# Three rounded products and centred weights in the expert up-projection of an RWKV and mixture-of-experts block

## What is computed

```python
# block 1: RWKV attention, per batch
key, value, rec = x mixed with x shifted by one token, three mixes
k, v = key @ Wk, value @ Wv
r = sigmoid(rec @ Wr)
rwkv = wkv(time_decay, time_first, k, v)      # a scan over the 512 tokens
x1 = layernorm(x + (r * rwkv) @ Wo)
# block 2: 8 experts of 16 hidden units, the best 2 of them per token
gate = softmax(x1 @ router_w.T) * top2_mask
a = silu(x1 @ down_w.T)                       # 128 hidden units per token
out = layernorm(x1 + (a * gate) @ up_w)       # up_w as a 128 x 512 matrix
```

## Time and profile before

| | |
|---|---|
| time, median of 3 runs | 491.31 us (491.24 to 491.47) |
| time of the profiled execution | 491.64 us |
| its span, first to last instruction | 489.7 us |
| mean granted clock of TensorE | 0.992 of full |
| busy: PE, PEld, DVE, ACT, POOL | 472.0, 315.8, 410.0, 339.9, 260.2 us |
| DMA traffic | 30.35 MB, mean 62 GB/s |

### The profile page before, as it was taken

How to read it: one execution, slowest core, us unless ns; L and a number is a source line. 1 busy time by engine, 2 the same in 40 slices (tenths; PEclk the granted TensorE clock), 3 DMA queues, 4 the chain that set the end, 5 groups by cost and what they waited for, 6 DMA issues and landing times. The chain is left out here.

```text
span 489.7 us, 6300 instructions
## 1 busy us (share of the span) xinstructions
PE 472.0 (96%) x1850; PEld 315.8 (64%) x1850; DVE 410.0 (84%) x655; ACT 339.9 (69%) x769; POOL 260.2 (53%) x279
## 2 busy tenths in 40 slices
PE   8998799999999999999999999999999999999992
PEld 3443366776776667776777668766676766777461
DVE  5998997897799887997799977998889977775687
ACT  1577456876767778875877788777777858747675
POOL 2455665466605866348735668159654483321326
PEclk9999899999999999999999999999999999999998
DMA  8800250002000032002220032100330011400015
GB/s 251 266 24 1 88 191 1 0 1 87 1 1 0 23 129 103 5 1 99 74 86 1 1 129 87 44 1 22 131 108 0 1 44 66 150 2 1 0 45 214
DMA packets 20098, 30.35 MB, mean 62 GB/s; under 512 B 2016, under 2 KB 7136, under 8 KB 20064
## 3 DMA queue, kind: packets, MB, share of 16 engines
q1 hardware_dynamic: 20064, 29.95, 18.7%
HBM read 21.56 MB, written 8.39 MB: 61 GB/s over the span
## 5 line engine op out<-in xcount | busy, mean ns | idle before, releaser
L514 ACT ACTIVATE PR<-PR 128x512 f32<-128x512 f32 x128 | 74.2, 580 | 46.9 <-PE PR L296 18.3
L320 PE MATMUL PP<-WO,RW 128*128 128x512 f32 x216 | 97.3, 592 | 0.0
L1030 POOL TENSOR_SCALAR NM<-SUM,RS 128x1 f32<-128x1 f32 x30 | 10.0, 334 | 153.4 <-ACT RS L514 153.4
L320 PEld LDWEIGHTS PP<-WO,RW 128*128 128x128 f32 x216 | 39.5, 190 | 39.3 <-issue 38.5
L1024 POOL TENSOR_TENSOR DQ<-DEN,EX 128x512 f32<-128x512 f32 x32 | 41.0, 1281 | 36.4 <-DVE DEN L734 36.4
L771 DVE TENSOR_TENSOR RW<-NU,PR 128x512 f32<-128x512 f32 x32 | 22.0, 687 | 41.5 <-ACT PR L514 41.5
L782 DVE SCALAR_TENSOR_TENSOR KT<-D,VEC,XT 128x512 f32<-128x512 f32 x56 | 53.0, 976 | 0.0
L514 ACT ACTIVATE EX<-PK 128x512 f32<-128x512 f32 x32 | 19.1, 596 | 44.3 <-DVE PK L727 43.6
L292 PE MATMUL PV<-VH,WVH 128*128 128x512 f32 x112 | 46.7, 417 | 0.9 <-DVE NU L758 0.9
L292 PE MATMUL PR<-RH,WRH 128*128 128x512 f32 x112 | 47.3, 422 | 0.2 <-DVE RW L771 0.2
L292 PE MATMUL PK<-KH,WKH 128*128 128x512 f32 x112 | 47.2, 421 | 0.0
(11 more groups left out here) (202 smaller groups left out, 1118.7 us busy)
## 6 DMA issues: line engine op xcount, KB each, us to landing
XT<-in_xt SPq DMA_DIRECT2D x32, 256.0 KB, 3.3
XN<-in_x SPq DMA_DIRECT2D x28, 256.0 KB, 2.7
out<-XN SPq DMA_DIRECT2D x28, 256.0 KB, 2.0
WO<-in_wo SPq DMA_DIRECT2D x1, 1024.0 KB, 7.3
XT<-in_x SPq DMA_DIRECT2D x4, 256.0 KB, 4.4
out<-XT SPq DMA_DIRECT2D x4, 256.0 KB, 2.1
X1T<-in_wk SPq DMA_DIRECT2D x2, 256.0 KB, 5.0
XN<-in_wv SPq DMA_DIRECT2D x2, 256.0 KB, 5.4
```

What stands on the lines that cost most here:

```text
L320: last = eng.matmul(projected_at(t), RW[(C * b + c) % NRW][:, 128 * n:128 * n + 128], WO[:, c, :], start=(c == 0), stop=(c == C - 1))
L514: eng.activation(*a, **k).then_inc(q[s], 1)
L1030: eng.tensor_scalar(NM1[:, col(t)], total, RS1[:, col(t)], scale, ALU.mult, ALU.mult)\
```

## The change

- The up weights are centred once: ScalarE sums each row of UP, GpSimd subtracts the mean. The product then has row mean zero, as has the normalised tile it is added to, so the second layernorm needs no mean: `residual2` is a plain add, `spread2` squares without a bias, and `normalise2` is one GpSimd operation, whose second scalar is a column of zeros.
- For tiles of batches 0 to 5 the up product is made in three fp32r terms. UP is split once into UPH and UPL (in slots 8 and 9), and the activations of each batch into AGH (ScalarE's copy, as before, now rounded) and AGL, by a new VectorE subtraction `gated_low`, that reads PSUM. Batches 6 and 7 keep the fp32 product.
- `MEASURED` falls from five tiles to the last three, `FINISHED` from two to one. Tiles of batch 6 are squared in pairs, with one Ln and one Exp for two.
- SCR is gone. WO holds the key mixes of batch 0, so its load waits for the last key product of batch 0; the activations' work space in the tail moves to M, DEN and NUM.

```diff
-        AGT = sb("AGT", [128, T])
+        AGH, AGL = sb("AGH", [128, T], F32R), sb("AGL", [128, T], F32R)
-        MEASURED = [NT * (LAST - 2) + 3, NT * (LAST - 1) + 1, NT * (LAST - 1) + 3, NT * LAST + 1, NT * LAST + 3]
+        MEASURED = [NT * LAST + 1, NT * LAST + 2, NT * LAST + 3]
-        FINISHED = [NT * LAST + 1, NT * LAST + 3]
+        FINISHED = [NT * LAST + 3]
...
-            load_w(WO, wo, "wo")
             load_w(DR, dr, "dr", 0, HD)
             eng.dma_start(TRI[:, :], tri).then_inc(q["tri"], 16)
+            eng.wait_ge(q["k"], C)
+            load_w(WO, wo, "wo")
...
+                if k < LAST - 1:
+                    eng.wait_ge(q["agl"], k + 1)
...
-                eng.matmul(up_at(t), PARTS[k].agt[:, o:o + 128], UP[:, :],
-                           start=True, stop=True).then_inc(q["up_"], 1)
+                if k < LAST - 1:
+                    eng.matmul(up_at(t), AGH[:, o:o + 128], UPH[:, :], start=True, stop=False)
+                    eng.matmul(up_at(t), AGH[:, o:o + 128], UPL[:, :], start=False, stop=False)
+                    last = eng.matmul(up_at(t), AGL[:, o:o + 128], UPH[:, :], start=False, stop=True)
+                else:
+                    last = eng.matmul(up_at(t), PARTS[k].agt[:, o:o + 128], UP[:, :], start=True, stop=True)
+                last.then_inc(q["up_"], 1)
...
+                if s == 2 * C:
+                    eng.wait_ge(q["up"], 16)
+                    act("upx", JUNK[:, :], UP[:, :], ACT.Copy, accum_out=SUMU[:, :])
+                if s == 2 * C + 1:
+                    eng.wait_ge(q["upc"], 1)
+                    act("uph", UPH[:, :], UP[:, :], ACT.Copy)
...
+            spread2(t5 + 3)
+            spread2(t6, 2)
+            spread2(t6 + 2, 2)
+            for t in range(t7, NT * NB):
                 spread2(t)
...
-                eng.scalar_tensor_tensor(out=xn_at(t), in0=up_at(t), scalar=1.0, in1=xn_at(t), op0=ALU.mult,
-                                         op1=ALU.add, accum_out=SUM2[:, col(t)]).then_inc(q["res2"], 1)
+                eng.tensor_tensor(xn_at(t), up_at(t), xn_at(t), ALU.add).then_inc(q["res2"], 1)
...
+            def gated_low(k):
+                eng.wait_ge(q["agc"], k + 1)
+                eng.tensor_tensor(AGL[:, :], PARTS[k].turned_at, AGH[:, :].bitcast(F32), ALU.subtract)\
+                   .then_inc(q["agl"], 1)
...
+                if j == 2 and s < U - 2 and batch(b - 2):
+                    gated_low(b - 2)
                 if j == 2 and b:
                     mixes(b + 1, 1, 0, 1)
...
-                i = MEASURED.index(t) if t in MEASURED else None
-                total, scale = (SUM2[:, col(t)], -1.0 / H) if i is None else (MV[:, i, 0:1], -1.0)
                 eng.wait_ge(q["rs2"], t + 1)
-                eng.tensor_scalar(NM2[:, col(t)], total, RS2[:, col(t)], scale, ALU.mult, ALU.mult)\
-                   .then_inc(q["nm2"], 1)
-                eng.wait_ge(q["nm2"], normalised(t))
-                eng.tensor_scalar(xn_at(t), xn_at(t), RS2[:, col(t)], NM2[:, col(t)], ALU.mult, ALU.add)\
+                eng.tensor_scalar(xn_at(t), xn_at(t), RS2[:, col(t)], ZERO[:, :], ALU.mult, ALU.add)\
                    .then_inc(q["nrm2"], 1)
...
+                if s == 2 * C:
+                    eng.wait_ge(q["upx"], 1)
+                    eng.tensor_scalar(NMU[:, :], SUMU[:, :], -1.0 / H, None, ALU.mult).then_inc(q["upm"], 1)
+                    eng.wait_ge(q["upm"], 1)
+                    eng.tensor_scalar(UP[:, :], UP[:, :], NMU[:, :], None, ALU.add).then_inc(q["upc"], 1)
+                if s == 2 * C + 1:
+                    eng.wait_ge(q["uph"], 1)
+                    eng.tensor_tensor(UPL[:, :], UP[:, :], UPH[:, :].bitcast(F32), ALU.subtract).then_inc(q["upl"], 1)
```

More of the change, by code:

```diff
@@ L47, in rwkv_moe_postln @@
         UP = sb("UP", [128, H])
+        UPH, UPL = sb("UPH", [128, H], F32R), sb("UPL", [128, H], F32R)
         IDN = sb("IDN", [128, 128])
@@ L74, in rwkv_moe_postln @@
         ST, MV = sb("ST", [128, 7, 6]), sb("MV", [128, 7, 2])
-        SUM2, SQ2, LV2, RS2, NM2 = (sb(n + "2", [128, 3 * NT]) for n in ("SUM", "SQ", "LV", "RS", "NM"))
+        SQ2, LV2, RS2 = (sb(n + "2", [128, 3 * NT]) for n in ("SQ", "LV", "RS"))
+        SUMU, NMU, ZERO = sb("SUMU", [128, 1]), sb("NMU", [128, 1]), sb("ZERO", [128, 1])
         PK = [bank("PK0"), bank("PK1")]
@@ L81, in rwkv_moe_postln @@
         TD, NTD, CC, QB = (CST[:, i, :] for i in range(4))
-        JUNK = SCR[:, 3, :]
         def full(b, which, c):
             if b == 0:
-                early = [AGT[:, :], UP[:, :]] + [h[:, :, :].rearrange("p n h -> p (n h)")[:, 0:T] for h in HS]
-                return (SCR[:, c, :], RW[C + c][:, :], early[c])[which]
+                early = [JUNK[:, :], UP[:, :]] + [h[:, :, :].rearrange("p n h -> p (n h)")[:, 0:T] for h in HS]
+                return (WO[:, c, :], RW[C + c][:, :], early[c])[which]
             if which == 2:
@@ L117, in __init__ @@
                 gm = spare[:, 768:780].rearrange("p (i n) -> p i n", i=3) if tail else GM
-                self.s1, self.s2 = (x[:, i, EI * lo:EI * hi] for i in range(2))
-                self.gt, self.eq = (x[:, 2 if tail else 1, o + E * E * lo:o + E * E * hi] for o in (0, 256))
+                s1, s2, pairs = (M, DEN, NUM) if tail else (X1T[:, 0, :], X1T[:, 1, :], X1T[:, 1, :])
+                self.s1, self.s2 = (a[:, EI * lo:EI * hi] for a in (s1, s2))
+                self.gt, self.eq = (pairs[:, o + E * E * lo:o + E * E * hi] for o in (0, 256))
                 self.hs = hs[:, lo:hi, :]
@@ L122, in __init__ @@
                 self.gm = [gm[:, i, lo:hi] for i in range(3)]
-                self.agt = (DQ if tail else NU if k == LAST - 1 else AGT)[:, 128 * lo:128 * hi]
+                self.agt = (DQ if tail else NU if k == LAST - 1 else AGH)[:, 128 * lo:128 * hi]
                 self.turned_at = ((PK[0], PH)[lo // 2] if tail else PP if k == LAST - 1 else PU)[:, 0:128 * (hi - lo)]
@@ L573, in spread, with spread2 @@
                 act("rs1", RS1[:, col(t)], LV1[:, col(t)], ACT.Exp, scale=-0.5)
-            def spread2(t):
+            def spread2(t, n=1):
+                cols = slice(col(t).start, col(t).start + n)
                 if t in MEASURED:
                     i = MEASURED.index(t)
-                    eng.wait_ge(q["mv2"], i + 1)
-                    act("lv2", LV2[:, col(t)], MV[:, i, 1:2], ACT.Ln, bias=EPS)
-                else:
[L581 to L587, removed]
+                    eng.wait_ge(q["mv2"], i + n)
+                    eng.activation(LV2[:, cols], MV[:, i:i + n, 1], ACT.Ln, bias=EPS).then_inc(q["lv2"], n)
+                else:
+                    for u in range(t, t + n):
+                        eng.wait_ge(q["res2"], u + 1)
+                        act("sq2", JUNK[:, :] if u == t else KT[0][:, :], xn_at(u), ACT.Square, accum_out=SQ2[:, col(u)])
+                    eng.wait_ge(q["sq2"], squared(t + n - 1, MEASURED))
+                    eng.activation(LV2[:, cols], SQ2[:, cols], ACT.Ln, bias=EPS, scale=1.0 / H).then_inc(q["lv2"], n)
+                eng.wait_ge(q["lv2"], t + n)
+                eng.activation(RS2[:, cols], LV2[:, cols], ACT.Exp, scale=-0.5).then_inc(q["rs2"], n)
             def turned(t):
@@ L710, in _ @@
             ffn_out(LAST + 1)
-            for t in range(t5 + 3, NT * NB):
+            spread2(t5 + 3)
+            spread2(t6, 2)
+            spread2(t6 + 2, 2)
+            for t in range(t7, NT * NB):
                 spread2(t)
@@ L946, in _ @@
                 if s == U - 1:
+                    gated_low(LAST - 2)
                     gate_scores(LAST - 1)
@@ L985, in _ @@
             silu(LAST + 1)
[L986 to L991, removed]
+            for n in range(NT):
+                residual2(t6 + n)
             residual2(t7)
-            moments2(t6 + 3)
             residual2(t7 + 1)
```

16 lines of the change are left out of this document (8 added, 8 removed), and 2 rows, old and new, of the table q.

## The result

| | changed | before |
|---|---|---|
| time, median | 490.16 us (489.48 to 491.82, 20 runs) | 491.35 us (490.81 to 492.47, 20 runs) |
| ratio, 95% interval | 0.9974 (0.9967 to 0.9981) | |
| profiled execution, its span | 489.89, 487.8 us | 491.64, 489.7 us |

The account below looks back on a forecast made before the run. The prediction took the ring of VectorE and ScalarE as the bound, TensorE following closely. Terms +2.6 - 1.0 + 1.0 - 0.8 = +1.8 us gave 493.1 us on the median; own range 492.2 to 494.3, 8-in-10 range 489.0 to 494.9.

Parts of the forecast that it names:

- The bound: In the loop: VectorE and ScalarE, not TensorE, set the batch period of 56.83 us, so TensorE's savings give nothing there.
- The ring of VectorE and ScalarE: Loop links between the two engines: `lead` to gates, `gate` to logarithm and exponential to `weigh`, mixes to highs; 56.83 us a batch.
- Rival 1: TensorE is the bound after all and its 4.1 us arrive: 486.8 us, chance 0.15; half arrives: about 489.5, chance 0.1.
- `gated_low` at 0: In j=2, five times, and slot 31: the new VectorE subtraction of 0.60 us was to cost 0 while covered.
- the cover named: In j=2: the mix behind `gated_low` waits anyway for the same GpSimd operation, which ends at 210.98.
- Rival 3: `gated_low` in j=2 isn't covered, five times 0.6 us on top: 496.1 us; chance 0.08.
- XN goes ahead of mix 2: In j=3, batches 2 to 6: GpSimd's norm gets in before the second mix, making it 0.52 us late; +2.6 us.
- Rival 2: In j=3 XN doesn't get in between the mixes: it asks later, or VectorE keeps the port; 490.5 us, chance 0.15.
- j=0, -1.0 us: In j=0, batches 3 to 6: XN, with two NM gone, ends before the first mix comes; -0.24 us each.
- UPL, +1.0 us: In slot 10, once: UPL in slot 9 pushes the lows back into the two mixes, `gate` 1.0 us late.
- The tail, -0.8 us: At the end: the last store leaves 0.8 us earlier, 0.44 of it from the up products; between 0 and -1.7.

Follow-up runs that it names:

- experiment 3: Changed kernel with only the first of the three fp32r terms in the up products of batches 0 to 5, and no `gated_low`: 489.06 us.
- experiment 4: Changed kernel with `gated_low` done three times instead of once in j=2 of batches 2 to 6: 494.4 us.
- experiment 5: Changed kernel with the second norm in j=3 as a GpSimd operation with two inputs, same result and place: 494.03 us.
- experiment 6: Changed kernel with a 128x1 GpSimd operation put back ahead of each second norm of batches 0 to 4: 490.55 us.
- experiments 7 and 8: Changed kernel with UP's centring and split moved from slots 8 and 9: to slots 5 and 8, 490.78 us; to slots 4 and 8, 488.81 us.
- experiment 2: Changed kernel with all up products in fp32, without `gated_low` or the split of UP; centred weights, norm and tail as changed: 489.29 us.
- experiment 9: Changed kernel with a column of zeros as the bias of the second block's squares: 490.44 us.
- experiment 1: The changed kernel run again, unedited: 490.23 us.

## Why the prediction was wrong

The forecast was +1.8 us, and the change gained 1.2. The measured 490.16 us lies in the wide range of 489.0 to 494.9, but not in the forecast's own of 492.2 to 494.3. One term failed, and the others came out nearly as worked out.

- **The bound: right.** The ring of VectorE and ScalarE sets the period; 4.0 us less on TensorE gave nothing in the loop, nor did 1.8 us less a batch (experiment 3), and VectorE's extra time appears in full once uncovered (experiment 4). Rival 1 is out.
- **`gated_low` at 0: right, by the cover named.** The mix behind it took 1.21 us instead of 1.82 and still waited for the same KL; 0.46 us of cover was left (experiment 4). Rival 3 is out.
- **"XN goes ahead of mix 2", +2.6 us: the step that failed.** It was worth 0. XN started early enough, at 224.44, 0.58 us before mix 1 ended, and still waited for both mixes. The prediction took the turn-taking from VL, a subtraction with two inputs, and applied it to the norm, which has one input and scalars. With two inputs it loses 0.75 to 0.79 us five times (experiment 5), even above the 0.52 of the forecast. Rival 2 had the outcome (490.5 us). Of its two reasons, "VectorE keeps it" fits. The other, that XN asks later than 0.45 us after its start, isn't settled: both forms start equally early, but no trace shows when an operation asks within its run. I also had the row that could have warned: the NM of the earlier trace rows, another one-input operation, waited for mix 1 and ended only 0.21 us after mix 2 had started, without having made mix 2 any longer. I took that for its being one element long. And the forecast looked at mix 2 alone: the mix that did lose, 1.03 us, is the third, which has slack.
- **j=0, -1.0 us: right**, -0.25 four times. The 128x1 step put back takes 0.64 of it away (experiment 6).
- **UPL, +1.0 us: right** in place and size, +1.04 (experiments 7 and 8).
- **The tail, -0.8 us: right in sign, too small: -1.29.** Behind slot 31 the copy comes 0.74 earlier, where 0.44 was taken. The products' part is 0.29, at the first gate (with fp32 products, experiment 2, the copy comes 0.30 later). The other 0.45 arises up to the second gate's end, 0.33 of it at one small operation that I hadn't looked at. It is L833 before, with its 0.60 us, and L855 now:

  Timeline of DVE and POOL in the tail of the kernel before:

```profile
472.73 0.26 POOL L1040 TENSOR_SCALAR NM<-SUM,RS 128x1 f32<-128x1 f32 x1 [4.25 <-ACT RS L514]
473.09 0.77 POOL L1043 TENSOR_SCALAR XN<-XN,RS,NM 128x512 f32<-128x512 f32 x1
...
473.28 0.60 DVE L833 TENSOR_TENSOR EX<-EX 128x16 f32<-128x16 f32 x1
```

  and in the changed kernel:

```profile
471.74 0.77 POOL L1059 TENSOR_SCALAR XN<-XN,RS,ZERO 128x512 f32<-128x512 f32 x1 [4.00 <-ACT RS L598]
...
472.26 0.27 DVE L855 TENSOR_TENSOR EX<-EX 128x16 f32<-128x16 f32 x1
```

  Without NM the norm ends at 472.51 instead of 473.86, and the gate's 128x16 operation no longer stands beside most of it. That this is why it is 0.33 shorter is read from the two traces; no run tests it. Behind the copy 0.55 us were gained where 0.36 was taken: the queue was laid out with squares of 0.71 us, and without a bias they take 0.62 (experiment 9).
- **The sum.** 0 - 1.0 + 1.04 - 1.29 = -1.25, against 1.19 between the medians. Without the failed step the prediction's own terms give 490.5.

## What to carry to other kernels

Before you price a collision of two engines, look for a row in which the same kind of operation meets the same kind; a subtraction's behaviour doesn't stand for a multiply by a scalar. An operation done once still costs in full if it pushes a queue into a tight place: look at the slot after the one where it stands, and after each move look again (experiments 7 and 8). And a busy share of 96% isn't a bound while the place of a batch in two traces stays put: take away some of that engine's work alone and see whether the period moves.

## What the runs showed of the hardware

**One input or two.** Beside back-to-back mixes on VectorE, GpSimd's one-input, 512-column operation waits through both (1.73 us), its two-input form goes in between them (1.49, and mix 2 then takes 1.52). The Trainium skill (GPSIMD Engine Reference, Key points) states that GpSimd and VectorE share SBUF interfaces; which of them goes first is what these rows add. The subtractions of the earlier trace rows have two inputs and nothing broadcast, and they take turns too. That the number of inputs decides, and not the length (a subtraction takes 1.27 us alone, the norm 0.77), is not shown.

**The start varies.** The program begins with ten dummy products of TensorE. Timeline of PE in the changed kernel:

```profile
4.15 1.06 PE L444 MATMUL PP<-RW 128*128 128x512 f32 x1
5.01 1.02 PE L444 MATMUL PP<-RW 128*128 128x512 f32 x1
5.86 0.60 PE L444 MATMUL PP<-RW 128*128 128x512 f32 x1
...
8.01 0.59 PE L280 MATMUL PK<-WO,X1T 128*128 128x512 f32 x1
```

They start 0.85 us apart, and from 5.86 us on 0.43 apart, a ratio of two, as between the clock's levels of 1.2 and 2.4 GHz, though here the granted clock reads 1.00 in all windows from 4 to 8 us (in experiment 1's slow stretch it reads 0.50). The first key product follows behind the tenth. It began at 8.01 and 7.54 us in two profiles of the changed kernel, at 8.70 and 8.55 in two of the kernel before, and between 7.25 and 8.48 in the ten others. In all 14 profiles the first dummy starts at 1.43 to 1.45 us, so what differs is when the spacing of 0.85 us gives way to 0.43: after two to five of them. The load of WO can't be the reason, since it was issued at 18.71 us before. So the 0.68 us between the first two profiles were left out of the account; that both profiles of before are at the late end stays unexplained, and the change's part in it, if any, open.

**A mix at the edge.** In experiment 2 the mixes of slot 6 took 3.60 us instead of 2.42, though they came 2.37 us after the first KL had started, and 2.36 in the changed kernel. Such a meeting can fall either way between two profiles, and here it is worth 1.2 us. It may fall either way between two executions of one kernel too: of the six times of experiment 2 three lie at 488.43 to 488.92 us and three, the profiled one among them, at 489.65 to 489.81; no second profile was taken to show it.
